# Pair 0 of a fused attention and MLP kernel: its loads on GpSimd's queue, other staging slots, an earlier shift flag, an earlier copy of the output weights

## The chip, the cores and the metric

One core of one Trainium2 chip. The metric is the device time of the kernel in microseconds (us), the median of the runs. Engines are named as in the profile: PE is TensorE (matmul), DVE is VectorE, ACT is ScalarE, POOL is GpSimd, SP is SyncE, which only issues transfers. "SPq" and "ACTq" are what an engine's own queue of instructions spends on issuing a transfer.

## The reference

```python
# x: (8, 1024, 512), H = 16 heads of 32, float32
y = layernorm(x)
q, k, v = split(y @ w_qkv)                       # per head; q and k are halved into q1,q2 and k1,k2
a = softmax(q1 k1^T / sqrt(32)) - lam * softmax(q2 k2^T / sqrt(32))
out = a @ v                                      # rms-normed over the 32 columns, times norm_w * 0.2
x = x + reshape(out) @ wo
z = layernorm(x)
h = bitlinear(z, w_fc) + gate * (z @ v.T @ fast_b.T @ u.T)   # bitlinear: ternary weights with a row scale
x = x + bitlinear(relu(h) ** 2, w_proj)
```

## The kernel before

Everything runs in one program with an order written out by hand for each engine; semaphores join them. Matmuls of float32 precision are made of three products of a high and a low part (`fp32r`).

**Opening.** The rows of x are taken in chunks of 512. For chunks 0 and 1 (batch 0) the kernel makes 24 "tiles" T = 0..23, twelve a chunk: eight tiles of q and k (numbered Q = 0..15 over both chunks) and four of v (V = 0..7). Each tile is 12 matmuls on PE (`pe_tile`, L822 for q and k, L825 for v) into one of four PSUM banks, T % 4, then a copy on ACT (`act_tile`), which takes the high part (L1286) or v (L1291), then for q and k the low part on DVE (`dve_low`, L1621) and the largest magnitude (`dve_bound`, L1631). SP then stores the tile into scratch tensors in DRAM (`sync_store`, L514 for q and k, L524 for v). Chunk 1 makes its tiles Q = 8..15 at T = 12..19 and V = 4..7 at T = 20..23. Between them PE also turns chunk 2 (`pe_turn`, ACT L1249, DVE L1571), and ACT and DVE quantize `w_fc`.

**The main loop** runs over 64 pairs of heads, P = 0..63, each in steps d = 0..7 of two score blocks. For block gg = 16 P + k, PE makes scores in two halves c = 0 and 1 (`pe_score`, L884; half 0 is in banks 0 and 1, half 1 in banks 2 and 3), ACT takes the exponential of each half (`act_exp`, L1308) into one of four slots of the tensor `pr`, gg % 4, DVE adds each block of a half pair to `acc` (`dve_add`, L1687, seven adds for eight blocks), and PE multiplies the block by v (`pe_pv`, L909). After seven adds PE sums `acc` over the partitions (`pe_sum`, L932). Between them lie the tiles of later batches (three tiles a pair from T = 24; tile 24 has six matmuls in d = 0 and six in d = 1), layer norm of a later chunk (DVE L1588: four statistics of chunk 3 in P = 0, d = 1), and the output projection of earlier pairs. The last stage is the MLP.

**What joins the opening to pair 0.** The scores of pair P read `qst` and `kst`, which are loaded from the scratch tensors by eight transfers (`sync_load_qk`, L552 and L554), and `pe_pv` reads `vst`, loaded in two halves (`sync_load_v`, L565): rows 0 to 3 of blocks before k = 0 is used, rows 4 to 7 before k = 4. In SP's order the q and k loads of pair 0 stand after the store of T = 15, the first half of v after T = 16, the second half after all 24 stores. Then come the loads of pair 1. A flag tells if pair 0 needs a shift of its scores against overflow: DVE takes the magnitudes (`dve_flag(0, 0)` after T = 19), PE spreads them (`pe_flag`, L839, inside T = 20), DVE makes the flag and zeroes `mh` (`dve_flag(0, 1)`, L1644 to L1651), and ACT issues four transfers from `mh` into two rows of `qst` (`sync_shift`, L576). The first score waits for these, for the loads, and for ACT's reads of all four PSUM banks (`s_v` at 8).

**Memory shared in time.** The eight staging slots `stp` of Q = 0..15 lie in the same SBUF memory as the four slots of `pr`: block gg = 0..3 of pair 0 overwrites staging slots 2 gg and 2 gg + 1. So `act_exp` for blocks 0 to 3 waits until the stores of the two tiles in these slots have landed. Before the change tile Q lies in slot (Q + 6) % 8:

```python
def stage(Q):
    return stp[:, (Q + 6) % STG] if Q < 16 else stg[:, Q % 2]
...
for slot in range(2 * gg, 2 * gg + 2):
    Q = STG + (slot + 2) % STG          # blocks 0..3: Q = 10,11 / 12,13 / 14,15 / 8,9
    stored(e, Q)
```

The output weights are cast on ACT by one instruction (L1443, `woh`) after the copy of tile T = 22, and DVE takes the low part (`wol`, L1849) before its first add. GpSimd fills rows of `kst` with ones at the start (slot 0) and after the fourth quantized unit (slot 1, L370); its next work is the layer norm of chunk 3 (L484).

Of the kernel before, what the change touches and what calls it, by code (L numbers as in the profile page):

```python
# [102 lines left out]
def build(nc, x, wqkv, wo, lq1, lq2, lk1, lk2, norm_w, fast_b, w_fc, w_proj, u, v, gate, out):  # L103
# [10 lines left out]
    with ExitStack() as top:  # L114
# [117 lines left out]
        with ExitStack() as al:  # L232
# [39 lines left out]
        s_shift = [sem(f"s_shift{k}") for k in range(RING)]  # L272
        s_va = [sem(f"s_va{k}") for k in range(RING)]
        s_vb = [sem(f"s_vb{k}") for k in range(RING)]
        s_wf = [sem(f"s_wf{k}") for k in range(4)]
# [38 lines left out]
                             "s_dn", "s_dfin", "s_fo", "s_res"))  # L314

        def stage(Q):

            return stp[:, (Q + 6) % STG] if Q < 16 else stg[:, Q % 2]

# [3 lines left out]

        def stored(e, Q):

            if Q < 16:
                e.wait_ge(s_stp[Q % STG], 32 * (Q // STG + 1))
            else:
                e.wait_ge(s_stg[Q % 2], 32 * (Q // 2 - 7))

# [20 lines left out]
        def gpsimd_program(e):  # L351
# [13 lines left out]
            for hh in range(2):  # L365
                e.wait_ge(s_pool, 7 + hh)
                e.memset(kst[64 * hh + 32:64 * hh + 64, 0, :, :].bitcast(F32), 1.0).then_inc(s_pool, 1)
            e.wait_ge(s_tern, 4)
            for hh in range(2):
                e.memset(kst[64 * hh + 32:64 * hh + 64, 1, :, :].bitcast(F32), 1.0).then_inc(s_k1, 1)  # L370

            for P in range(LOWP - 1):
                if P - 1 in JOINED:
                    join_halves(e, P - 1)
                if SUM_P <= P < PROJ_P:
                    pool_magnitudes(e, 2 * (P - SUM_P))
                if PROJ_P <= P < PROJ_P + 16:
                    pool_ternary(e, P - PROJ_P)
                pool_part_apply(e, P)
                if SUM_P <= P < PROJ_P:  # L380
                    pool_magnitudes(e, 2 * (P - SUM_P) + 1)
                if P - 1 in POOLED:
                    pool_normed(e, P - 1)
                if P == PROJ_P + 16:
                    e.wait_ge(s_tts, 16 * 24)
                    e.memset(fba[:], 0.0).then_inc(s_pool, 1)
# [116 lines left out]
        def sync_store_qk(e, b, c, i):  # L503
            m, Q = TILES[i], (2 * b + c) * 8 + i
            sc = (qsc if m < 4 else ksc)[b % 2, m % 4]
            e.wait_ge(s_qh, Q + 1)
            e.wait_ge(s_ql, Q + 1)
            if c == 0 and b >= 2:

                last = (b - 2) * NP + 2 * (m % 4)  # L510
                e.wait_ge(s_ring[last % 2], 128 * (last // 2 + 1))
                e.wait_ge(s_ring[(last + 1) % 2], 128 * ((last + 1) // 2 + 1))
            for part in range(2):
                e.dma_start(sc[:, part, :, c * 512:(c + 1) * 512], stage(Q)[:, part, :].bitcast(F32)) \  # L514
                    .then_inc(s_stp[Q % STG] if Q < 16 else s_stg[Q % 2], 16)

        def sync_store_v(e, b, c, st):
            t, V = 4 * c + st, (2 * b + c) * 4 + st
            e.wait_ge(s_v, V + 1)
            if b >= 2 and t in (0, 4):  # L520
                last = (b - 1) * NP - 1
                for r in range(RING):
                    e.wait_ge((s_vb if t else s_va)[r], 16 * ((last - 1 + (last - 1 + r) % 2) // 2 + 1))
            e.dma_start(vsc[b % 2, :, t].rearrange("p q d -> p (q d)"), stage_v(V)).then_inc(s_vsg[V % 2], 16)  # L524
# [8 lines left out]

        def sync_load_qk(e, P):
            b, q = divmod(P, NP)
# [12 lines left out]
            for dst, sc, both, again in ((qst, qsc, 0, 32), (kst, ksc, 16, 0)):  # L548
                for hh in range(2):
                    rows = sc[b % 2, tile, s0 + 2 * hh:s0 + 2 * hh + 2]  # L550
                    r0, r1 = 64 * hh + both, 64 * hh + again
                    e.dma_start(dst[r0:r0 + 32, r, :, :].bitcast(F32), rows.rearrange("j c d s -> (c d) j s")) \  # L552
                        .then_inc(s_ring[r], 16)
                    e.dma_start(dst[r1:r1 + 16, r, :, :].bitcast(F32), rows[:, 0].rearrange("j d s -> d j s")) \  # L554
                        .then_inc(s_ring[r], 16)

        def sync_load_v(e, P, half):
            b, q = divmod(P, NP)
# [4 lines left out]
            if P >= RING:  # L563
                e.wait_ge(s_pv, 16 * (P - RING) + 16)
            e.dma_start(vst[:, r, t0:t0 + 4, :], vsc[b % 2, :, t0:t0 + 4, q, :]).then_inc((s_vb if half else s_va)[r], 16)  # L565

# [116 lines left out]
        def sync_program(e):  # L683
# [12 lines left out]
            for T in range(24):  # L696
# [7 lines left out]
                if T in (10, 22):  # L704
                    sync_x(e, 2 if T == 10 else 3)
                if T == 15:
                    sync_load_qk(e, 0)
                if T == 16:
                    sync_load_v(e, 0, 0)
            sync_load_v(e, 0, 1)  # L710
            for P in range(NPAIR):
                w, more = P // 4, 3 * P + 24 < 24 * B
                for d in range(8):
                    if d == 0 and P + 1 < NPAIR:
                        sync_load_qk(e, P + 1)
                    if d == 6 and P + 1 < NPAIR:
# [3 lines left out]
                    if d in (2, 7) and P + 1 < NPAIR:  # L720
                        sync_load_v(e, P + 1, d // 7)
                    if d == 7 and w + 4 < NC + 2:
# [123 lines left out]
        def pe_shift(e, flag, P):  # L846

            r, base_pe, base_dve, b0 = P % RING, 33 * P, 34 * P, shift_bank(P)
            with e.If(flag > 0):
                e.wait_ge(s_ring[r], 128 * (P // RING + 1))  # L850
                if P:
# [20 lines left out]
        def pe_score(e, P, k, c):  # L872
            gg, j, t, r = 16 * P + k, k // 8, k % 8, P % RING
            if k == 0 and c == 0:
                e.wait_ge(s_ring[r], 128 * (P // RING + 1))
                e.wait_ge(s_shift[r], 64 * (P // RING + 1))
            if gg:
                e.wait_ge(s_exp, n_half(gg - 1, c))
            elif c == 0:
                e.wait_ge(s_ql, 16)  # L880
                e.wait_ge(s_v, 8)
            for hh in range(2):
# [5 lines left out]
        def pe_pv(e, gg):  # L888
# [3 lines left out]
            if k == 0:  # L892
                e.wait_ge(s_va[r], 16 * (P // RING + 1))
            if k == 4:
                e.wait_ge(s_vb[r], 16 * (P // RING + 1))
            if t == 0:
# [373 lines left out]
        def act_tile(e, T, bk):  # L1270
            C, i = kind_of(T)
            e.wait_ge(s_tile, T + 1)
            if i < 8:
                Q = C * 8 + i
                if Q < 16:
                    if Q == 2:
                        e.wait_ge(s_wl, 8)
                    if Q >= STG:
                        stored(e, Q - STG)
                        e.wait_ge(s_qx, Q - STG + 1)  # L1280
                elif Q >= 18:
# [11 lines left out]
        def act_exp(e, P, k, c):  # L1293
# [3 lines left out]
            if c == 0:  # L1297
# [4 lines left out]
                else:  # L1302

                    for slot in range(2 * gg, 2 * gg + 2):
                        Q = STG + (slot + 2) % STG
                        stored(e, Q)
# [104 lines left out]
        def scalar_program(e):  # L1411
# [9 lines left out]
            for T in range(24):  # L1421
# [15 lines left out]
                if T - 2 in UNIT_AT:  # L1437
                    act_ternary(e, UNIT_AT.index(T - 2))
                if T == 22:
                    e.wait_ge(s_wo, 16)  # L1440
# [357 lines left out]
        def vector_program(e):  # L1798
# [16 lines left out]
            for T in range(24):  # L1815
# [24 lines left out]
                if T == 19:  # L1840
                    dve_flag(e, 0, 0)
                if 0 <= k < 4:
                    dve_turn(e, C + 1, k, 4 + k)
                if T == 20:
                    dve_flag(e, 0, 1)
                    flag = load_flag(e, 0)
                    dve_shift(e, flag, 0)
            e.wait_ge(s_woh, 1)
            e.tensor_tensor(wol[:], wos, woh[:], ALU.subtract).then_inc(s_wol, 1)  # L1849
# [163 lines left out]
```

## Time and profile before

| | us |
|---|---|
| median of 3 runs | 3742.93 (3742.35 to 3745.72) |
| profiled execution | 3746.0 |
| its span (first to last instruction) | 3743.9 |
| PE busy in the span | 3704.6 (99%) |
| DVE / ACT / POOL busy | 3149.4 / 2789.7 / 721.1 |
| granted TensorE clock, mean | 0.998 |

Times of rows are microseconds from the span's start. A busy row of PE can hold waits inside: matmuls are pipelined and their ends are modelled. The profiled execution's time is the span and 2.1 us around it.

### The profile page before, as it was taken

To read this page: it belongs to the slowest core of one execution; us is meant where nothing else is said; L and a number is where in the kernel's file an instruction comes from. 1 tells how busy PE (TensorE), PEld (TensorE's weight loads), DVE (VectorE), ACT (ScalarE), POOL (GpSimd) and SP (SyncE) were. 2 spreads that over 40 slices of the span, in tenths; PEclk is the share of its full clock that TensorE was granted. 3 is DMA by queue.
4 is the path that set the end of the run, shared out by engine and by line. 5 is a ranking of instruction groups with operands and counts; after the bars stand their busy time and mean duration, and the time that the engine had idled before them with its cause. 6 is when DMAs were issued, how large, how long until landed. Compare 5 with 4: busy or idle time off the path is not lost.

```text
span 3743.9 us, 57714 instructions
## 1 busy us (share of the span) xinstructions
PE 3704.6 (99%) x21736; PEld 2054.7 (55%) x21736; DVE 3149.4 (84%) x2886; ACT 2789.7 (75%) x3614; POOL 721.1 (19%) x325
## 2 busy tenths in 40 slices
PE   8999999999999999999999999999999999999999
PEld 6344444444444444444444444444468888888887
DVE  6899999999999999999999999988875555555554
ACT  4898888988888888888888888889873333333333
POOL 0101101024545445234332401320020000000000
PEclk9999999999999999999999999999999999999999
DMA  7544444445444544554555444544340101010010
GB/s 241 133 102 102 107 104 104 105 99 111 101 101 103 110 106 99 111 112 104 116 110 116 98 98 103 128 93 114 78 152 23 46 23 46 23 45 23 29 40 23
DMA packets 247207, 344.58 MB, mean 92 GB/s; under 512 B 118048, under 2 KB 126240, under 8 KB 245856
## 3 DMA queue, kind: packets, MB, share of 16 engines
q1 hardware_dynamic: 243360, 324.43, 36.8%
q0 software_dynamic: 3392, 15.73, 1.3%
q8 instruction: 208, 3.41, 0.4%
q14 instruction: 119, 0.97, 0.1%
q10 hardware_dynamic: 128, 0.03, 0.0%
HBM read 198.55 MB, written 131.07 MB: 88 GB/s over the span
## 4 chain that ended last, share of the span: by engine, by line
PE 92%; DVE 4%; issue 1%; ACT 1%; SPq 1%; DMA 0%; DVEq 0%; ACTq 0%
PE ps L909 23%; PE ps L884 17%; PE ps L978 13%; PE ps L1036 12%; PE ps L822 9%; PE ps L964 5%; PE ps L825 4%; PE ps L932 3%; DVE acc L1687 3%; PE ps L983 2%; PE ps L786 1%; PE ps L1072 1%; PE ps L945 1%; ACT pr L1308 1%; PE ps L1057 1%
## 5 line engine op out<-in xcount | busy, mean ns | idle before, releaser
L1308 ACT ACTIVATE pr<-ps 128x1024 f32<-128x1024 f32 x2048 | 1989.7, 1029 | 261.0 <-PE ps L884 252.1
L1687 DVE TENSOR_TENSOR acc<-acc,pr 128x2048 f32<-128x2048 f32 x768 | 1788.3, 2328 | 43.6 <-ACT pr L1308 14.6
L909 PE MATMUL ps<-pr,vst 128*32 128x512 f32 x8192 | 1009.1, 598 | 0.0
L884 PE MATMUL ps<-qst,kst 50*128 50x512 f32 x4096 | 781.2, 456 | 11.5 <-ACT pr L1308 9.7
L884 PEld LDWEIGHTS ps<-qst,kst 50*128 50x128 f32 x4096 | 336.9, 184 | 659.3 <-ACT pr L1308 462.7
L909 PEld LDWEIGHTS ps<-pr,vst 128*32 128x32 f32 x8192 | 213.1, 109 | 445.8 <-issue 437.8
L1478 ACT ACTIVATE rb<-ps,scf 128x512 f32<-128x512 f32 x228 | 157.1, 689 | 349.5 <-PE ps L983 349.5
L1036 PE MATMUL ps<-tP,hh_ 128*128 128x512 f32 x1024 | 399.4, 390 | 1.4 <-DVE hl_ L1911 1.4
L1036 PE MATMUL ps<-tP,hl_ 128*128 128x512 f32 x1024 | 398.8, 389 | 0.0
L822 PE MATMUL ps<-xt,wqh 128*128 128x512 f32 x1024 | 379.3, 423 | 1.4 <-ACT xt L1253 0.8
L484 POOL TENSOR_SCALAR xin<-xin,mv,rs 128x512 f32<-128x512 f32 x60 | 206.5, 3445 | 868.1 <-DVE rs L1606 868.1
L978 PE MATMUL ps<-yh,tT 128*128 128x512 f32 x896 | 350.9, 392 | 0.0
L978 PE MATMUL ps<-yl,tT 128*128 128x512 f32 x896 | 348.7, 389 | 0.0
L1687 DVE TENSOR_TENSOR acc<-pr 128x2048 f32<-128x2048 f32 x128 | 294.7, 2302 | 52.2 <-ACT pr L1308 49.6
L822 PEld LDWEIGHTS ps<-xt,wqh 128*128 128x128 f32 x1024 | 191.3, 191 | 118.9 <-issue 81.6
L1036 PEld LDWEIGHTS ps<-tP,hh_ 128*128 128x128 f32 x1024 | 192.2, 188 | 43.5 <-DVE hl_ L1911 2.3
L1036 PEld LDWEIGHTS ps<-tP,hl_ 128*128 128x128 f32 x1024 | 192.2, 188 | 39.9 <-issue 0.2
L822 PE MATMUL ps<-xt,wql 128*128 128x512 f32 x512 | 203.7, 399 | 0.0
L1906 DVE TENSOR_TENSOR sb2a<-rb 128x512 f32<-128x512 f32 x114 | 78.8, 691 | 137.2 <-ACT rb L1478 137.2
L825 PE MATMUL ps<-wqh,xt 128*128 128x512 f32 x512 | 190.0, 417 | 0.0
L978 PEld LDWEIGHTS ps<-yl,tT 128*128 128x128 f32 x896 | 168.3, 188 | 34.1
L978 PEld LDWEIGHTS ps<-yh,tT 128*128 128x128 f32 x896 | 168.2, 188 | 34.1
(183 smaller groups left out, 3900.1 us busy)
## 6 DMA issues: line engine op xcount, KB each, us to landing
qst<-q_scratch SPq DMA_DIRECT2D x128, 256.0 KB, 4.6
kst<-k_scratch SPq DMA_DIRECT2D x128, 256.0 KB, 7.1
q_scratch<-stg SPq DMA_DIRECT2D x112, 256.0 KB
k_scratch<-stg SPq DMA_DIRECT2D x112, 256.0 KB
qst<-q_scratch SPq DMA_DIRECT2D x128, 128.0 KB, 5.0
kst<-k_scratch SPq DMA_DIRECT2D x128, 128.0 KB, 7.6
vst<-v_scratch SPq DMA_DIRECT2D x128, 128.0 KB, 4.8
xr<-in_L_attn_x_dram SPq DMA_DIRECT2D x64, 256.0 KB
```

The lines of the kernel that those rows point to most:

```text
L484: e.tensor_scalar(xin[:, st, :], xin[:, st, :], mv[:, st, 0:1], rs[:, 8 + st:9 + st], ALU.subtract, ALU.mult) \
L822: t = e.matmul(ps[:, bk, :], w[:, k, m0:m0 + 128], xx[:, k, :], start=(n == 0), stop=(n == 11))
L825: t = e.matmul(ps[:, bk, :], xx[:, k, st * 128:(st + 1) * 128], w[:, k, 2 * E:3 * E], start=(n == 0), stop=(n == 11))
L884: ins = e.matmul(ps[:, 2 * c + hh, :], kst[rows, r, j, t * 128:(t + 1) * 128], qst[rows, r, j, c * 512:(c + 1) * 512], start=True, stop=True)
L909: ins = e.matmul(ps[32 * c4:32 * c4 + 32, 4 + j, :], vst[:, r, t, 32 * hh:32 * hh + 32], pr[:, sl, c, hh, :], start=(t == 0), stop=(t == 7 ...
L932: t = e.matmul(ps[32 * c4:32 * c4 + 32, sum_bank(X, j), :], ones[:], acc[:, j, (2 * c + hh) * 512:(2 * c + hh + 1) * 512], start=True, sto ...
L964: t = e.matmul(ps[:, 7, :], o_[:, kk, :], w_[:, kk, :], start=(kk == 0 and i == 0), stop=(kk == 3 and i == 2))
L978: t = e.matmul(ps[:, bk, :], tT[:, i, m // 2, :], (hi, lo)[m % 2][:, m // 2, :], start=(m == 0), stop=False)
L1036: t = e.matmul(ps[:, rt, :], h_[:, uu % 3, rt * 128:(rt + 1) * 128], tP[:, i, :], start=(i == 0 and part == 0), stop=(i == 15 and part == 1))
L1308: e.activation(pr[:, sl, c, :, :], ps[:, 2 * c:2 * c + 2, :], ACT.Exp, scale=SCALE).then_inc(s_exp, 1)
L1478: e.activation(rb[:, uu % 2, :], ps[:, 4 + uu % 2, :], ACT.Relu, scale=scf[:, 0, i:i + 1]) \
L1687: e.tensor_tensor(acc[:, j, :], old, new, ALU.add).then_inc(s_add, 1)
```

## The change

Four edits that belong to the opening and pair 0:

1. **Slots.** Tiles Q = 8..15 lie in slots 0..7 in order, so blocks 0..3 of pair 0 wait for the stores of Q = 8,9 / 10,11 / 12,13 / 14,15. Tiles Q = 0..7 keep their slots; a tile of chunk 1 waits for the tile of chunk 0 that had its slot.
2. **Loads of pair 0.** GpSimd issues the eight loads of q and k and the first half of v after it has filled slot 0 of `kst` with ones, and the second half of v after it has filled slot 1. They have semaphores of their own. SP issues none of them; after the 24 stores it goes on to the loads of pair 1.
3. **Flag.** In DVE's step T = 20 the flag and `mh` come before the turn of chunk 2's last quarter, not behind it.
4. **Output weights and banks.** ACT casts `wo` after T = 21 instead of T = 22. The first score's half 0 waits for ACT's reads of banks 0 and 1 only (`s_v` at 6), half 1 for all (8).

```diff
+        def ring_of(P):
+            return (s_ring[P % RING], 128 * ((P + 1) // RING)) if P else (s_first, 128)
+        def values_of(P, half):
+            return ((s_vb if half else s_va)[P % RING], 16 * ((P + 1) // RING)) if P else (s_vfirst[half], 16)
+        def slot_of(Q):
+            return Q - STG if Q >= STG else (Q + 6) % STG
         def stage(Q):
-            return stp[:, (Q + 6) % STG] if Q < 16 else stg[:, Q % 2]
+            return stp[:, slot_of(Q)] if Q < 16 else stg[:, Q % 2]
...
         # gpsimd_program, behind the ones of kst slot 0
+            load_qk(e, 0)
+            load_v(e, 0, 0)
             e.wait_ge(s_tern, 4)
             for hh in range(2):
                 e.memset(kst[64 * hh + 32:64 * hh + 64, 1, :, :].bitcast(F32), 1.0).then_inc(s_k1, 1)
+            load_v(e, 0, 1)
...
         # sync_program
-                if T == 15:
-                    sync_load_qk(e, 0)
-                if T == 16:
-                    sync_load_v(e, 0, 0)
-            sync_load_v(e, 0, 1)
...
         # pe_score
             elif c == 0:
                 e.wait_ge(s_ql, 16)
+                e.wait_ge(s_v, 6)
+            else:
                 e.wait_ge(s_v, 8)
...
         # act_tile
                     if Q >= STG:
-                        stored(e, Q - STG)
-                        e.wait_ge(s_qx, Q - STG + 1)
+                        last = (slot_of(Q) + 2) % STG
+                        stored(e, last)
+                        e.wait_ge(s_qx, last + 1)
...
         # act_exp, blocks 0 to 3
                     for slot in range(2 * gg, 2 * gg + 2):
-                        Q = STG + (slot + 2) % STG
+                        Q = STG + slot
                         stored(e, Q)
                         e.wait_ge(s_qx, Q + 1)
...
         # scalar_program: the cast of wo
-                if T == 22:
+                if T == 21:
...
         # vector_program
                 if T == 19:
                     dve_flag(e, 0, 0)
-                if 0 <= k < 4:
-                    dve_turn(e, C + 1, k, 4 + k)
                 if T == 20:
                     dve_flag(e, 0, 1)
                     flag = load_flag(e, 0)
                     dve_shift(e, flag, 0)
+                if 0 <= k < 4:
+                    dve_turn(e, C + 1, k, 4 + k)
```

The rest of the diff gives the waits on `s_ring`, `s_va` and `s_vb` their new form (`ring_of`, `values_of`), renames `sync_load_qk` and `sync_load_v` to `load_qk` and `load_v`, and numbers `s_stp` by slot.

## Rows read from the trace of the kernel before

**Rows 1.** The page: the span and the first engine's busy time.
```profile
span 3743.9 us, 57714 instructions
...
PE 3704.6 (99%) x21736; PEld 2054.7 (55%) x21736; DVE 3149.4 (84%) x2886; ACT 2789.7 (75%) x3614; POOL 721.1 (19%) x325
```

**Rows 2.** The chain that ended last, 65 to 125 us: start, us, what.
```profile
97.47 9.97 DMA k_scratch<-stp
```

**Rows 3.** PE's timeline: start, duration, instruction, count, idle time before and its releaser.
```profile
97.12 0.39 PE L825 MATMUL ps<-wqh,xt 128*128 128x512 f32 x1
99.22 0.73 PE L884 MATMUL ps<-qst,kst 50*128 50x512 f32 x4 [1.72 <-DMA qst<-mh]
100.83 0.50 PE L884 MATMUL ps<-qst,kst 50*128 50x512 f32 x2 [0.88 <-ACT pr L1308]
...
103.78 1.22 PE L884 MATMUL ps<-qst,kst 50*128 50x512 f32 x4
...
118.05 1.92 PE L909 MATMUL ps<-pr,vst 128*32 128x512 f32 x16
...
128.88 1.06 PE L932 MATMUL ps<-acc,ones 128*32 128x512 f32 x8
```

**Rows 4.** ACT's timeline around the first exponentials.
```profile
92.39 2.63 ACTq L576 DMA_DIRECT2D qst<-mh  x4
...
96.09 1.92 ACT L1443 ACTIVATE woh<-acc 128x2048 fp32r<-128x2048 f32 x1
...
102.49 1.02 ACT L1308 ACTIVATE pr<-ps 128x1024 f32<-128x1024 f32 x1 [0.80 <-DMA k_scratch<-stp]
104.61 1.02 ACT L1308 ACTIVATE pr<-ps 128x1024 f32<-128x1024 f32 x1 [1.10 <-PE ps L884]
107.62 2.94 ACT L1308 ACTIVATE pr<-ps 128x1024 f32<-128x1024 f32 x3 [1.99 <-DMA k_scratch<-stp]
```

**Rows 5.** DVE's timeline, from tile 15's low part to the third add of pair 0.
```profile
85.82 0.69 DVE L1621 TENSOR_TENSOR stp<-ps,stp 128x512 fp32r<-128x512 f32 x1 [1.31 <-ACT stp L1286]
...
87.42 0.68 DVE L1571 TENSOR_TENSOR xt<-ps,xt 128x512 fp32r<-128x512 f32 x1
...
91.18 0.27 DVE L1651 MEMSET mh<- 32x256 f32 x1
...
105.67 2.29 DVE L1687 TENSOR_TENSOR acc<-pr 128x2048 f32<-128x2048 f32 x1 [5.34 <-ACT pr L1308]
109.59 2.29 DVE L1687 TENSOR_TENSOR acc<-acc,pr 128x2048 f32<-128x2048 f32 x1 [1.63 <-ACT pr L1308]
112.88 0.69 DVE L1621 TENSOR_TENSOR stg<-ps,stg 128x512 fp32r<-128x512 f32 x1 [0.99 <-ACT stg L1286]
...
115.86 2.27 DVE L1687 TENSOR_TENSOR acc<-acc,pr 128x2048 f32<-128x2048 f32 x1
```

**Rows 6.** SP's timeline: the last stores of the opening and the loads behind them.
```profile
100.68 0.62 SPq L489 DMA_DIRECT2D xin<-in_L_attn_x_dram  x1
101.34 2.35 SPq L524 DMA_DIRECT2D v_scratch<-stg  x1
112.66 0.37 SPq L565 DMA_DIRECT2D vst<-v_scratch  x1
```

**Rows 7.** Loads of half of v (L565), 0 to 140 us, and their time to landing.
```profile
L565 SPq DMA_DIRECT2D vst<-v_scratch x4: 370/392/573, 89.2 to 135.8; - x4
...
DMA to landing us min/median/max: 2.5/5.5/10.6
```

**Rows 8.** GpSimd's own transfers late in the kernel: issue times, and landing of the four.
```profile
2416.26 2.37 POOL L401 DMA_DIRECT2D tT<-tt_scratch  x4
...
DMA to landing us min/median/max: 11.3/15.0/18.4
...
L473 POOL DMA_DIRECT2D rbl<-r_scratch x28: 536/536/584, 2732.7 to 2797.7; - x28
```

**Rows 9.** Windows: stretch, length, busy of the engines, granted clock, DMA share, GB/s.
```profile
100.00:110.00 10.00, 6.95 (x25) 3.39 (x26) 3.03 (x3) 6.12 (x7) 0.00 (x0) 0.75 0.88 306
```

## The prediction before the run

> **What bounds the kernel now.** I read the page first: PE is busy 3704.6 of 3743.9 us [rows 1], so in the long middle nothing but less PE work or less PE idling helps, and the change removes no matmul. What it can win lies in the 39.3 us that PE is not busy, and in matmuls that run slowly. The change touches only the seam between the opening and pair 0, so I went on to the chain of work that ended last, in the stretch 65 to 125 us. It runs on SP's queue, which issues one store of q and k after another with other transfers between them, until the last one, of tile 15, has been issued at 97.47 and takes 9.97 us to land [rows 2]. Then it jumps to ACT.
>
> The ACT timeline shows why. The exponential of block 2 writes where tile 15 is staged, and starts at 107.62, after an idle 1.99 us put down to that store; block 1 had waited 0.80 us for tile 13's store at 102.49 [rows 4]. PE's timeline shows the same from its side: the tiles end at 97.12 + 0.39 = 97.51, the first score starts at 99.22 after 1.72 us for the transfer of `mh`, and there are waits again later [rows 3]. In the window 100 to 110 us PE is busy 6.95 of 10 us, at a mean granted clock of 0.75, between the two levels of 1.2 and 2.4 GHz; PE had idled just before [rows 3, 9].
>
> The DVE timeline tells what the lost time is worth. Its first add starts at 105.67 after 5.34 us of idling, the second at 109.59 after 1.63, the low part of tile 24 at 112.88 after 0.99, and from there DVE works without a gap through the third add at 115.86 [rows 5] up to PE's sum at 128.88 [rows 3], which needs the seventh add. From the sum on, PE is full. So the gain is how much earlier DVE reaches the third add with its blocks ready.
>
> **The change part by part.**
>
> *Flag.* `dve_turn` of the last quarter (0.68 us, as its like in [rows 5]) and the wait for ACT ahead of it are taken from the flag's way. PE's flag matmuls were over at about 88.2, DVE's turn of the third quarter ends at 87.42 + 0.68 = 88.1. The zeroing of `mh` starts 91.18 [rows 5]; three small instructions stand ahead of it (0.56 us), so it can start at 88.25 + 0.56 = 88.8. ACT issues the four transfers 1.21 us behind that start now (92.39 against 91.18), so at 90.0, where ACT is just through with its copy for the turn. They take 2.63 us [rows 4], to 92.65, and the last now lands at about 99.2, 4.8 us after its own issue at 94.3 [rows 3, 4]; then at 96.8. That is ahead of PE's 97.51. The first score's limit becomes the end of the tiles. Cost: the turn of the last quarter comes perhaps 0.5 us later, in a stretch where DVE idles for microseconds; without that cover it would be 0.5 us.
>
> *Output weights and banks.* The cast of 1.92 us stands now at 96.09 [rows 4], ahead of the copy of the last tile. Behind T = 21 it starts at 92.65 + 0.6 = 93.25 and ends 95.2, in ACT's idle time. V = 6 follows at 95.2, V = 7 when PE is through at 97.55, to 98.15. Half 0 of the first score can start at 97.5, half 1 at 98.2. `wol` on DVE (2.29 us) ends at 97.5, well before any add. All of this is hidden; the visible part is the 1.6 us by which the first exponential moves: 98.15 instead of 99.75.
>
> *Slots.* Blocks 1 and 2 no longer wait for tiles 13 and 15. Block 3 waits for tile 15. Its low part is ready at 86.5 (the row at 85.82 lasts 0.69 [rows 5]), and SP is free of the nine loads that it issued between 81.08 and 89.6, so I take its issue at 87 to 90 in place of 97.47; with the 9.97 us of [rows 2] it lands by 100. Block 3 starts near 105.4, so this wait goes away, with 5 us to spare. In the opening, tiles 8 to 15 now wait for other tiles of chunk 0; the tightest is tile 13 at 73 for tile 7, whose store was issued at 56.45 to 57.6. With the 9.97 us it lands by 67.6. Cost nothing.
>
> *From there to the third add.* Exponentials take 1.02 us, some 0.95 back to back. Block 0: 98.15 and 99.1. Block 1, half 0: 100.0. For half 1, PE has the score of half 0 at 99.25 (when block 0's half is read), six matmuls of tile 24, then the score. That took 103.78 - 100.83 = 2.95 us plus 0.83 to the exponential at 104.61 [rows 3, 4], at the lower clock for most of it. At the higher clock the six are 1.0 us shorter. PE's idle times ahead shrink from 2.60 us (1.72 + 0.88 in [rows 3]) to about 0.8, so I take the middle: 99.25 + 3.3 = 102.5, ends at 102.0 and 103.0. First add: 103.5 (now 105.67). Second add: 103.5 + 2.29 = 105.8 (block 2 is ready at 105.4). Tile 24's copy on ACT comes at about 107.2, so DVE's low part starts when the second add ends, at 108.1, where now 112.88. The four statistics need x of chunk 3: its load is issued at about 96.4 instead of 100.68 [rows 6] and took 11.4 us, so 107.8, in time. The third add starts 2.98 us after the low part, as now (115.86 - 112.88): 111.1. That is 4.8 us less; by the ends of the clock term 4.3 to 5.3.
>
> *Loads on GpSimd.* No load from this queue at this place exists in the trace. The nearest rows: 28 transfers of 256 KB at 0.54 us an issue, and four of 1 MB issued in 2.37 us, one behind another without waiting for a landing of 11.3 to 18.4 us [rows 8]. Tile 9's store has landed by 81.0, as SP did not wait for it then; by the latest GpSimd issues nine loads from 81.0 to 86. From below, landing as on SP now (3.5 to 9.3 us): 95.3. From above, the 18.4 of [rows 8]: 104.4, which is 6.9 us late. I take the first: the 18.4 belongs to transfers four times as large that queued behind each other. The ones of `kst` slot 1 (3.66 us) move behind these loads, to about 90; they are needed for pair 1's loads after 99. SP's queue loses about 8 us of issuing, and gives it to the stores, as used above. POOL's next work, at 130, is far.
>
> *The second half of v.* Now SP waits 5.7 us for V = 7's store, issued 101.34 and landed after 11.3 us, and issues at 112.66; it lands in 2.5 us, at 115.2; block 4 needs it at about 119 (second half of the row at 118.05) [rows 3, 6, 7]. After: V = 7 is stored at 98.3, lands between 106.5 (a landing of 8) and 109.6 (11.3), GpSimd adds 0.6, the load 2.5 to 10.6 [rows 7]. So it lands between 109.6 and 120.8, and is needed at 119 - 4.8 = 114.2. New is that pair 1's eight loads (1.5 MB), so far behind that wait, are now issued at once behind V = 7 and run beside it. With the median of 5.5 I get 112.6 to 115.7, a wait of 0 to 1.5 us. I charge 0.4.
>
> A rule speaks against this part. In [rows 5] DVE is in an add nearly all the time from 103 on, an instruction with two operands in SBUF. The Trainium skill (SBUF — State Buffer, "Who interferes with whom") says that GpSimd can't write its descriptors while DVE holds the port pair they share; it counts two-operand adds as takers of the read side only and infers that descriptors pass. By that inference the sum stands; if the adds did block, the issue would wait for the end of one add, up to 2.29 us more, and the gain would be about 2.5. No row here has both at once.
>
> **Sum.** 4.8 - 0.4 = 4.4 us. Against the profiled execution, 3746.0, that is 3741.6; that one was 3.1 above the median, so from the median, 3742.93, I forecast **3738.5**. Of this kernel 0.2% is 7.5 us, about what a measurement can tell from no change, and the forecast is within it.
>
> **The rivals.**
> *A. As worked out*, PE's first sum at about 124.5 in place of 128.88: 3737.5 to 3739.6. Chance 0.57.
> *B. The second half of v takes the place of the wait removed.* For it: pair 1's loads beside it and a DMA share of 0.88 at this time now [rows 9]. Against: x is issued earlier too. At a landing of 120.8 PE would wait 6.6 us at block 4, and the whole comes out 1.8 us above now: 3744.7; half way, 3741.4. Chance 0.25 for 3739.6 to 3744.7.
> *C. Slower: GpSimd's loads are late for the first score.* Needed at 97.5; from 99.22 on it loses against now. At the 18.4 us of [rows 8], 104.4: the start is 5.2 later than now, less the 3.2 us that slots still give (4.8 less the 1.6 of the start): +2.0, 3744.9. If each had to land (4.4 us, the median of those 28) before the next is issued, nine take 44 us and the start is at 125: +22.6, 3765.5. For it: nothing in the opening tests that queue. Against: four in flight at once in [rows 8]. It passes 0.2% from a start at 110 on. Chance 0.08, of which 0.05 beyond 0.2%.
> *D. More than forecast*, because PE's clock stays up and ACT and DVE find more slack: the first add can't start before 103, so by DVE's own work 5.3 is the limit, 3737.6; less only by run to run variation. Beyond it, by something I don't see: 0.10, a fifth of it beyond 0.2%.
>
> **How the numbers follow.** The likeliest is A, 3738.5. With A and B's nearer part, and about 1.5 us for how medians of such runs differ, 8 in 10 lie from 3736.3 to 3742.8. Faster by over 0.2% (below 3735.4): 0.04, from D and variation. Slower by over 0.2% (above 3750.4): 0.05, from C. Within: 0.91.
>
> **What would show it.** Right: no wait of ACT L1308 for `k_scratch<-stp`; ACT's four issues at about 90; the first score at 97.6; adds at 103.5, 105.8, 111.1; the first L932 at 124.5; the granted clock of 100 to 110 above 0.75. Wrong: PE L909 waiting for `vst` near 114 (B); the first score waiting for `qst` or `kst` loads (C); DVE's statistics waiting for `xin`.

## The result and the profile after

| | before | after |
|---|---|---|
| median, 22 runs each | 3743.34 | 3748.45 |
| lowest to highest | 3741.18 to 3746.96 | 3746.09 to 3753.35 |
| profiled execution / its span | 3746.0 / 3743.9 | 3748.61 / 3746.9 |

The ratio is 1.0013, 95% interval 1.0008 to 1.0019. The kernel is 5.1 us slower, where 4.4 us faster was forecast. It is less than the 0.2% that a measurement was taken to tell, but with 22 runs it is clear of zero. The two profiled executions differ by less, 2.6 us, because that of the kernel before ran 2.7 us over its median and that of the kernel after 0.2.

PE's timeline of the kernel after (the first score, the products with v of blocks 3 and 4 with the wait between them, the first sum; L895, L920 and L943 answer to L884, L909 and L932 of [rows 3]):

```profile
96.28 0.50 PE L895 MATMUL ps<-qst,kst 50*128 50x512 f32 x2
...
110.42 1.07 PE L920 MATMUL ps<-pr,vst 128*32 128x512 f32 x8
120.36 1.94 PE L920 MATMUL ps<-pr,vst 128*32 128x512 f32 x8 [8.88 <-DMA vst<-v_scratch]
...
131.47 1.04 PE L943 MATMUL ps<-acc,ones 128*32 128x512 f32 x8
```

PE starts the first score 2.9 us sooner than in [rows 3] and, at block 3's product (110.42), is 7.6 us ahead of 118.05. Then it stands still for 8.88 us, for the second half of v, and makes the first sum at 131.47 instead of 128.88. DVE's timeline after has the same turn, with another wait in it:

```profile
101.57 2.29 DVE L1699 TENSOR_TENSOR acc<-pr 128x2048 f32<-128x2048 f32 x1 [5.21 <-ACT pr L1320]
103.97 2.29 DVE L1699 TENSOR_TENSOR acc<-acc,pr 128x2048 f32<-128x2048 f32 x1
106.18 0.68 DVE L1633 TENSOR_TENSOR stg<-ps,stg 128x512 fp32r<-128x512 f32 x1
112.56 2.47 DVE L1600 BATCH_NORM_STATS2 st<-xin 128x6 f32<-128x512 f32 x4 [5.70 <-DMA xin<-in_L_attn_x_dram]
114.94 2.27 DVE L1699 TENSOR_TENSOR acc<-acc,pr 128x2048 f32<-128x2048 f32 x1
```

The queues show where both come from. SP's timeline after, then GpSimd's:

```profile
96.77 0.43 SPq L503 DMA_DIRECT2D xin<-in_L_attn_x_dram  x1
97.25 1.31 SPq L538 DMA_DIRECT2D v_scratch<-stg  x1
98.81 0.39 SPq L566 DMA_DIRECT2D qst<-q_scratch  x1
...
102.25 0.44 SPq L568 DMA_DIRECT2D kst<-k_scratch  x1
```

```profile
78.66 0.50 POOL L568 DMA_DIRECT2D kst<-k_scratch  x1
91.76 0.81 POOL L579 DMA_DIRECT2D vst<-v_scratch  x1 [12.61 <-issue]
92.61 3.66 POOL L383 MEMSET kst<- 32x2048 f32 x2
113.52 0.76 POOL L579 DMA_DIRECT2D vst<-v_scratch  x1 [17.25 <-DMA v_scratch<-stg]
```

Tile V = 7's store is issued at 97.25, 4.1 us sooner than in [rows 6]. Pair 1's eight loads follow at 98.81 to 102.7; in [rows 6] SP was stuck until 112.66 and they came behind that. Now the store takes 15.9 us to land (11.3 before), the load of x 15.8 (11.4 before), GpSimd can issue at 113.52, and its load lands 6.7 us later, at 120.2. The store lands 0.6 us behind x (112.0 and 112.6 before, 112.5 and 113.1 now). The windows (their last three columns: granted clock, DMA share, GB/s) show the transfers' side and the price on the clock:

```profile
100.00:105.00 5.00, 4.62 (x27) 2.14 (x26) 3.32 (x2) 4.14 (x5) 0.00 (x0) 1.00 1.08 314
105.00:110.00 5.00, 5.00 (x34) 2.39 (x32) 1.86 (x2) 4.00 (x5) 0.00 (x0) 1.00 1.09 157
110.00:115.00 5.00, 1.48 (x12) 0.20 (x10) 2.44 (x5) 1.94 (x2) 0.76 (x1) 0.95 0.95 127
115.00:120.00 5.00, 0.00 (x0) 0.00 (x0) 4.96 (x9) 0.50 (x2) 0.00 (x0) 0.50 0.58 172
120.00:125.00 5.00, 4.64 (x16) 1.89 (x16) 3.58 (x3) 1.94 (x2) 0.00 (x0) 0.53 0.17 56
```

The DMA engines are full from 100 to 115 us. During PE's standstill the granted clock falls to 0.50, the lower level of 1.2 GHz, and stays there into the next window (0.53); the eight matmuls at 120.36 take 1.94 us where eight at 110.42 took 1.07.

### The profile page after: what moved, and what is told of

The parts are those of the page before. It is cut to its first block, busy times and chain, and to the rows that moved or that the text cites. A ratio compares the mean times of both kernels' runs of the same rounds, so it can differ in the third digit from the quotient of the medians.

```text
span 3746.9 us, 57714 instructions
## 1 busy us (share of the span) xinstructions
PE 3704.0 (99%) x21736; PEld 2054.0 (55%) x21736; DVE 3149.4 (84%) x2886; ACT 2790.5 (74%) x3614; POOL 728.9 (19%) x335
## 4 chain that ended last, share of the span: by engine, by line
PE 90%; DVE 5%; issue 2%; ACT 1%; DMA 1%; ACTq 0%; SPq 0%; DVEq 0%; POOLq 0%
PE ps L920 23%; PE ps L895 17%; PE ps L989 13%; PE ps L1047 12%; PE ps L831 9%; PE ps L975 5%; PE ps L834 4%; DVE acc L1699 4%; PE ps L943 3%; PE ps L994 2%; PE ps L795 1%; PE ps L1083 1%; PE ps L956 1%; PE ps L1068 1%; ACT pr L1320 1%
## 5 line engine op out<-in xcount | busy, mean ns | idle before, releaser
L920 PE MATMUL ps<-pr,vst 128*32 128x512 f32 x8192 | 1010.2, 599 | 8.9 <-DMA vst<-v_scratch 8.9
L895 PE MATMUL ps<-qst,kst 50*128 50x512 f32 x4096 | 781.5, 456 | 7.4 <-ACT pr L1320 7.1
L895 PEld LDWEIGHTS ps<-qst,kst 50*128 50x128 f32 x4096 | 337.1, 184 | 655.7 <-ACT pr L1320 458.8
L920 PEld LDWEIGHTS ps<-pr,vst 128*32 128x32 f32 x8192 | 213.0, 109 | 455.0 <-issue 444.5
```

The source lines that it names most:

```text
L895: ins = e.matmul(ps[:, 2 * c + hh, :], kst[rows, r, j, t * 128:(t + 1) * 128], qst[rows, r, j, c * 512:(c + 1) * 512], start=True, stop=True)
L920: ins = e.matmul(ps[32 * c4:32 * c4 + 32, 4 + j, :], vst[:, r, t, 32 * hh:32 * hh + 32], pr[:, sl, c, hh, :], start=(t == 0), stop=(t == 7 ...
```

## The experiments

Two theories at first. **Theory 1**: the order costs the time. SP's own load of the second half of v, which waited for V = 7's store, held back pair 1's loads; with it on GpSimd they start 10 us early and slow that store and what comes after it. **Theory 2**: GpSimd's queue is slow by itself. "First sum" is the start of pair 0's first L932 (or its line in that kernel) in the one profiled execution; "median" stands against that of the kernel before beside it, measured in the same set. The ratio is the record's own for the runs of both kernels; it is not the quotient of the two medians.

| kernel | first sum | median, its before | ratio (95%) |
|---|---|---|---|
| before | 128.9 | | |
| after | 131.5 | 3748.45, 3743.34 | 1.0013 (1.0008 to 1.0019) |
| e1_gate | 125.5 | 3741.99, 3744.18 | 0.9998 (0.9989 to 1.0007) |
| e2_all_sp | 125.1 | 3743.34, 3744.18 | 1.0001 (0.9992 to 1.0010) |
| e3_gpsimd_only | 130.3 | 3748.75, 3744.18 | 1.0014 (1.0005 to 1.0023) |
| e4_v2_sp | 124.1 | 3739.51, 3744.18 | 0.9988 (0.9979 to 0.9997) |
| e5_x_early | 123.2 | 3740.43, 3743.29 | 0.9997 (0.9988 to 1.0006) |
| e6_slots_only | 124.6 | 3742.98, 3743.29 | 1.0002 (0.9993 to 1.0011) |
| e7_v7_first | 128.1 | 3746.09, 3743.29 | 1.0009 (1.0000 to 1.0018) |
| e10_sp_order | 133.0 | 3750.84, 3743.82 | 1.0020 (1.0011 to 1.0029) |
| e12_gate_landed | 122.1 | 3741.42, 3743.82 | 0.9993 (0.9984 to 1.0002) |
| e13_flag_banks | 126.1 | 3745.83, 3743.82 | 1.0006 (0.9997 to 1.0015) |
| e15_gate_landed_2 | 124.0 | 3740.53, 3743.79 | 0.9991 (0.9982 to 1.0000) |
| e16_v2_sp_2 | 122.0 | 3741.14, 3743.79 | 0.9993 (0.9984 to 1.0002) |
| e17_all_sp_2 | 128.1 | 3743.16, 3743.79 | 0.9994 (0.9985 to 1.0003) |

**e1_gate.** After, with SP held until V = 7's store has landed:

```diff
         # sync_program, behind the 24 stores
+            e.wait_ge(s_vsg[1], 64)
+            e.wait_ge(s_vsg[0], 64)
             for P in range(NPAIR):
```

> The changed kernel, and SP waits for the stores of v (tile V = 7) before it issues pair 1's loads, as it did by its place in the order before. Theory 1 (pair 1's 1.5 MB, issued at 98.8 us right behind V = 7, slow its store from 11.3 to 15.9 us): the store lands about 11 us after 97.3, so at 108 to 109, GpSimd's load of the second half of v lands by 113 to 116, PE waits 0 to 3 us for it instead of 8.9, the first L932 of pair 0 comes at 125 to 127 and the median is 3738 to 3741. Theory 2 (GpSimd's path is slow by itself, the store's landing is not pair 1's doing): the store still takes 15 to 16 us, PE waits 8 to 9 us, 3748.

The store took 12.2 us instead of 15.9, GpSimd issued at 108.48, v landed 5.5 us later, PE waited 3.4 us for it instead of 8.9. The wait list of PE in e1_gate, 90 to 140 us (total, times, longest):

```profile
PE ps L897 <- ACT pr L1322: 3.7, 8, 0.9
PE ps L922 <- DMA vst<-v_scratch: 3.4, 1, 3.4
```

For theory 1. With two added waits on SP the median is 2.2 us below that of the kernel before, where the change had put it 5.1 above; by its interval e1_gate is no different from the kernel before.

**e2_all_sp.** Edits 1, 3 and 4; all of pair 0's loads on SP at their old places (`load_qk(e, 0)` after T = 15, `load_v(e, 0, 0)` after T = 16, `load_v(e, 0, 1)` after the stores).

> Edits 1, 3 and 4 alone: slots, flag, weights and banks; SP issues all loads of pair 0 at their old places. Theory 1: SP's own load of the second half of v gates pair 1's loads again; SP's backlog returns too (V = 7's store at 98 to 101). PE waits 0 to 2 us for v, first L932 at 125 to 127, 3738.5 to 3741. Theory 2 expects the same here: it can't be told apart by this run. A third theory, that the time is lost elsewhere in the three edits: 3746 or more.

The profile came as forecast, the median hardly moved. So the other three edits don't lose the 5 us; what they gain is less than forecast. e17 returns to it.

**e3_gpsimd_only.** Edit 2 alone; slots, flag, weights and banks as before.

> Edit 2 alone on the kernel before: GpSimd issues pair 0's loads, slots, flag, weights and banks stay. Theory 1: stores are issued earlier (no wait of ACT for tile 15), but pair 1's loads come behind V = 7 at once; second half of v lands at about 120, PE waits for it some 5 to 8 us, 3746 to 3750. Theory 2: the same. If the loss needs the other three edits: 3740 to 3743.

Slower by 4.6 us: nearly the whole loss is in this one edit. V = 7's store took 14.8 us, PE waited 5.2 us for v.

**e4_v2_sp.** After, with one line moved back:

```diff
         # gpsimd_program
-            load_v(e, 0, 1)
...
         # sync_program, behind the 24 stores
+            load_v(e, 0, 1)
```

> The changed kernel, with only the second half of v back on SP at its old place, ahead of pair 1's loads; GpSimd issues q, k and the first half. Theory 1: as e1_gate, and 0 to 3 us sooner by the landing (2.5 us before): PE waits 0 to 1.5 us, first L932 at 124.5 to 126, 3737.5 to 3740. Theory 2 (GpSimd's path): also good, but then e1_gate stays at 3748. So the pair e1_gate and e4_v2_sp tells them apart.

Its interval leaves 1 out, at 0.9988: the best median of all (in its second set, e16_v2_sp_2, the interval holds 1). GpSimd still issues nine of pair 0's ten loads, so these do no harm beyond a wait of 0.5 us for the first of PE's products with v, which starts at 99.95, when the first half of v has just landed (99.9). SP's timeline shows the old order again, with the second half of v ahead of pair 1:

```profile
97.09 2.46 SPq L537 DMA_DIRECT2D v_scratch<-stg  x1
109.30 0.37 SPq L578 DMA_DIRECT2D vst<-v_scratch  x1
109.91 0.54 SPq L565 DMA_DIRECT2D qst<-q_scratch  x1
```

The store took 12.2 us, the load 2.1.

**e5_x_early, e7_v7_first.** The load of chunk 3's x is moved in SP's order (`if T in (10, 22)` becomes `(10, 20)` on e4_v2_sp and `(10, 23)` on the kernel after).

> e4_v2_sp (second half of v back on SP ahead of pair 1's loads) with the load of chunk 3's x issued after T = 20 instead of T = 22. In e4_v2_sp DVE waited 2.2 us for that load and its first L932 came at 124.1. If the transfers' order alone sets these waits: x lands about 3 us sooner, DVE's wait is gone, V = 7's store lands as before (12 us after its issue), first L932 at 122.5 to 124, median 3737.5 to 3739.5. If the queue is simply full at this time: V = 7 lands later by as much as x lands sooner, the second half of v is late instead, 3739.5 to 3742.

> The changed kernel, with chunk 3's x load issued after V = 7's store instead of before it; pair 1's loads still follow at once, and GpSimd loads the second half of v. If V = 7's store is late because of what is issued behind it (pair 1's 1.5 MB): it still takes 13 to 16 us, v lands at 117 or later, PE waits 6 us or more, DVE waits longer for x, 3747 to 3751. If it is late because of the 1 MB of x ahead of it: it lands by 106 to 108, v by 112 to 115, PE waits 0 to 3 us, and 3741 to 3745.

In e5_x_early DVE no longer waited for x, the first sum was at 123.2, and the median no different from e4_v2_sp's by more than they scatter. In e7_v7_first both my branches were half right: V = 7's store landed in 6.9 us, with pair 1's loads and x behind it, and GpSimd could issue at 104.46. So the store is quick without x ahead of it. x itself still took 14.6 us, beside pair 1's loads. But the load of v, issued beside pair 1's loads, then took 12.3 us instead of 6.7, PE waited 5.3 us, DVE 5.1 for x, and the kernel stayed slower. So pair 1's loads cost twice: they lengthen x's load, behind which V = 7's store lands, and GpSimd's load of v. In e7_v7_first the first packet of that load started only at 113.0, 8.6 us after its issue, against 1.5 to 2.0 us in the other runs; what held it there is not shown.

**e12_gate_landed, e15_gate_landed_2.** One step beyond e1_gate; SP waits until the second half of v has landed:

```diff
+            e.wait_ge(s_vfirst[1], 16)
             for P in range(NPAIR):
```

> The changed kernel, all of pair 0's loads on GpSimd, and SP holds pair 1's loads until the second half of v has landed, not only until tile V = 7 is stored (e1_gate, where v took 5.5 us to land and PE waited 3.4). Theory 1 in its second part (pair 1's loads also slow GpSimd's load of v beside them): v lands in 3 to 4 us, PE waits 0.5 to 2 us, first L932 at 124 to 125.5, 3739 to 3742. If the 5.5 us are GpSimd's own: PE waits 3.4 us as in e1_gate, 3742.

> e12_gate_landed once more. Its profile had the first L932 at 122.1, 6.8 us ahead of the kernel before, but its median was only 2.4 us lower. If the saved time stays to the end and the first median was chance: 3737 to 3740. If part of it is given back later in the timed runs: 3740.5 to 3742.5 again.

GpSimd's load landed in 3.2 us and PE didn't wait for it; in e15_gate_landed_2 it landed in 2.7 us and PE waited 0.7 us. The waits of PE in e12_gate_landed, 90 to 150 us, and its window 105 to 110:

```profile
PE ps L896 <- ACT pr L1321: 3.1, 7, 0.9
PE ps L944 <- DVE acc L1700: 1.2, 1, 1.2
```

```profile
105.00:110.00 5.00, 5.00 (x34) 2.43 (x32) 4.97 (x7) 3.82 (x5) 0.76 (x1) 1.00 0.15 46
```

The DMA share is 0.15 where it was 1.09 in the kernel after, and theory 2 is out: this is GpSimd's queue, all ten loads on it, in its best order, with medians 2.4 and 3.3 us below that of the kernel before (each interval still reaches 1). It is as good as e4_v2_sp within what these runs can tell.

**e10_sp_order.** The converse: no load on GpSimd at all (e2_all_sp), but SP issues pair 1's loads ahead of pair 0's second half of v:

```diff
-            load_v(e, 0, 1)
             for P in range(NPAIR):
...
                     if d == 0 and P + 1 < NPAIR:
                         load_qk(e, P + 1)
+                        if P == 0:
+                            load_v(e, 0, 1)
```

> No load on GpSimd: edits 1, 3 and 4, all loads of pair 0 on SP, but pair 1's eight loads are issued ahead of pair 0's second half of v, so they no longer wait for tile V = 7's store. Theory 1 (the order, not GpSimd, costs the time): V = 7's store takes 14 us or more instead of 10.8 (e2_all_sp), the second half of v lands at 117 or later, PE waits 5 us or more for it, first L932 at 128 or later, 3746 to 3750. Theory 2 (GpSimd's queue is the cause): as e2_all_sp, first L932 at 125, 3741 to 3744.

7.0 us slower than the kernel before, the slowest of all. SP and PE in e10_sp_order:

```profile
95.76 2.34 SPq L535 DMA_DIRECT2D v_scratch<-stg  x1
98.34 0.50 SPq L563 DMA_DIRECT2D qst<-q_scratch  x1
...
111.65 0.38 SPq L576 DMA_DIRECT2D vst<-v_scratch  x1
```

```profile
119.39 1.94 PE L923 MATMUL ps<-pr,vst 128*32 128x512 f32 x8 [8.65 <-DMA vst<-v_scratch]
```

The store took 15.9 us again, the load of v 7.6, and PE waited 8.65 us, without GpSimd. This is the cause on its own.

**e6_slots_only, e13_flag_banks.** The other edits by themselves, all loads on SP: edit 1, and edits 3 and 4.

> Edit 1 alone (slots), all loads of pair 0 on SP as in the kernel before. By my sum the slots are worth 4.8 less the 1.6 us that the earlier start gives, 3.2 us: first score at 99.2 after a wait for the transfers of the shift rows, no wait for tile 15's store, first L932 at 126 to 127, median 3740 to 3742. If flag, weights and banks carry the gain: as the kernel before, 3743 to 3744.

> Edits 3 and 4 alone (flag, output weights, banks); slots as before, all loads on SP. The first score comes at about 97.6 or sooner, but block 2 still waits for tile 15's store at about 105 to 107.5, so by my sum nearly nothing reaches the first L932: 127 to 129, 3742 to 3744. If these edits carry a gain of their own: 125 to 126.5.

Slots alone gave a first sum at 124.6, earlier than I had them (126 to 127), yet a median within 0.3 us of that of the kernel before; the part on the prediction says how the two go together. Flag, weights and banks alone started the first score early and then waited for tile 15's store, in ACT's wait list of e13_flag_banks (95 to 125 us):

```profile
ACT pr L1322 <- DMA k_scratch<-stp: 2.9, 2, 2.7
```

A first sum at 126.1, a median 2.0 us higher with an interval that holds 1. No gain of their own.

**e8_v_first, e14_q_v_k.** GpSimd's order: first half of v first, or between the q and the k loads. They ask why that load was held 12.61 us in the kernel after.

> The changed kernel with GpSimd's first load of v ahead of its eight loads of q and k. In the changed kernel that load, ninth on the queue, was issued 12.6 us behind the eighth, just after the eighth had landed, with no wait of its own left. Theory: the queue had no room for its 512 pieces of 256 bytes until the loads ahead had landed. Then here v is issued at about 75 and the last of the eight loads wait for it (several us of idling between issues, the last issued at 82 or later). If the 12.6 us belong to the v load itself (a late store), v comes at 75 or later without delay, and the eight follow back to back, the last at 80 to 81.

> The changed kernel with GpSimd's first load of v between its four loads of q and its four of k. In e8_v_first, v went first at 66.8 without delay and the eight followed back to back after it had landed; in the changed kernel, ninth behind eight in flight, it was held 12.6 us. Theory (the queue has room for only so many pieces in flight): v behind four in flight is held until those four have landed or nearly so (6 to 9 us, issued at 80 to 84), or it fits, and then the loads of k are held. If instead v is never held behind four and k follows at once, room is not the reason.

In e8_v_first it was issued at 66.8, before the tiles for q and k were stored; it had landed (75.6) before the third of the eight went out, they followed back to back, and nothing was held. My times for it were wrong, and it shows only that its own wait is over by 66.8. In e14_q_v_k v went fifth without delay, and the ninth load, one of k, was held. GpSimd's timeline of e14_q_v_k:

```profile
75.25 0.80 POOL L580 DMA_DIRECT2D vst<-v_scratch  x1
76.03 0.54 POOL L567 DMA_DIRECT2D kst<-k_scratch  x1
...
87.07 0.51 POOL L569 DMA_DIRECT2D kst<-k_scratch  x1 [9.48 <-issue]
```

So the ninth load waits, whichever it is, and not for a semaphore of its own. That it lacks room in the queue is argued, and what counts as room is open: in e14_q_v_k the first load had landed at 78.0, and the hold went on until 87.07, 0.4 us after the landing of v (86.7), with one load of k still under way. Both kernels kept the fault of the change, one run each: 3749.5 and 3746.8.

**e16_v2_sp_2, e17_all_sp_2.** e4_v2_sp and e2_all_sp again.

> e4_v2_sp once more: 4.7 us lower by its median, first L932 4.8 us ahead. If the median follows the first sum, again 3738.5 to 3740.5, and ahead of e15 by nothing or behind it by 1 to 2 us.

> e2_all_sp once more. Its profile had 1.6 us more than the kernel before between the first and the second L932, in a stretch where the granted clock fell to 0.72 (140 to 145 us). If that belongs to this kernel: again, first L932 at 125, second at 146.5 to 147, 3742 to 3743.5. If it comes and goes from run to run: second L932 at 145.3 in this profile, or the median at 3739.5 to 3741.5.

e4_v2_sp was lower by 4.7 and 2.7 us in its two sets, e2_all_sp by 0.8 and 0.6, e12_gate_landed by 2.4 and 3.3. The first sums of two executions of one kernel differ by 2 to 3 us (e2_all_sp 125.1 and 128.1, e4_v2_sp 124.1 and 122.0): one profile doesn't fix them closer. And what is saved at the first sum doesn't always stay. e2_all_sp's windows before its second sum, and e4_v2_sp's for the same stretch:

```profile
140.00:145.00 5.00, 5.00 (x25) 1.74 (x22) 4.78 (x3) 2.27 (x4) 0.00 (x0) 0.72 0.98 180
```

```profile
140.00:145.00 5.00, 5.00 (x38) 2.27 (x34) 4.40 (x4) 3.65 (x4) 0.00 (x0) 1.00 0.99 179
```

The granted clock fell to 0.72 in the one and not in the other. From the first to the second sum it is 21.9 us in both profiles of e2_all_sp, 21.7 to 21.9 in e1_gate, e8_v_first, e13_flag_banks, e14_q_v_k and e15_gate_landed_2, and 20.2 to 20.3 in before, after, e3_gpsimd_only, e4_v2_sp twice, e5_x_early, e6_slots_only, e7_v7_first, e10_sp_order and e12_gate_landed. That is 1.6 us given back. It doesn't belong to a kernel: e12_gate_landed and e15_gate_landed_2 are the same, and the clock of 140 to 145 us was 1.00 in the one (20.2 us) and 0.70 in the other (21.7 us). So it is not shown to be the reason why e2_all_sp gains less than e4_v2_sp; and in their second sets the ratios, 0.9994 and 0.9993, don't tell the two apart.

## Why the prediction was wrong

- **Which part bound the kernel**: right. The seam between the opening and pair 0 moved with the store of tile 15. After the change no wait of ACT for it is left in 95 to 125 us.
- **Flag, weights and banks**: right. ACT's four issues came at 88.88 (90.0 forecast), the first score at 96.28 (97.5), half 1 at 97.03 behind ACT's read. The opening of that execution was itself 1.2 us shorter, so this is the forecast to 0.1 us.
- **Slots, to the third add**: the forecast had adds at 103.5 and 105.8, measured 101.57 and 103.97, low part 106.18 (108.1). The third add, forecast at 111.1, came at 114.94, behind the wait for x. PE's clock stayed at 1.00 through 110 us; I had halved that term.
- **The loads of q, k and the first half of v on GpSimd** cost nothing in the kernel after, as forecast: those of q and k were issued from 74.9 to 79.2, the last landed by 91.4, before the first score. The first half of v was held, issued at 91.76, and landed at 97.5; PE used it from 100.63 on. The margin is small: in e4_v2_sp the hold cost 0.5 us. Rival C fell.
- **The step that failed is "The second half of v"**: its landing of V = 7 in 8 to 11.3 us, and the charge of 0.4 us. The upper bound came from an execution in which nothing stood behind that store. I named what was new, that pair 1's eight loads now follow at once, and then left it out of both the store's landing and x's: 15.9 and 15.8 us. PE waited 8.88 us where I had 0 to 1.5, so the charge should have been the whole forecast gain and more. e10_sp_order and e12_gate_landed show the cause from both sides. The term that the loads lengthen first is x: in all 15 runs with x right ahead of V = 7 the store landed 0.6 to 0.8 us behind x, and with x behind it (e7_v7_first) it took 6.9 us. I also misread how long SP stood: two waits of 5.7 and 3.2 us, 8.9 in all and not 5.7.
- **x of chunk 3** was called in time at 107.8; DVE waited 5.70 us for it, to 112.56. The same omission, at the same place.
- **Rival B** was the right one, and its worst case priced too low. Its landing of 120.8 was met (120.2). Its wait of 6.6 us was 8.9, because PE got there at 111.5 and not at 114.2: the better the other edits work, the longer this wait. And it had no term for the clock: 0.50 to 0.53 from 115 to 125 us. At the first sum this is 0.8 us more than its worst case (131.47 against 128.88 + 1.8). The larger part of the way from 3744.7 to 3748.45 is the base: the rows of before, and their first sum, are of an execution 2.7 us over its median, while I set what I had worked out from them against the median. I gave it 0.25, and the range ended at 3742.8 although this case reached 3744.7.
- **The rule on GpSimd's descriptors and DVE** was not in play at the load for which I raised it. GpSimd issued the second half of v at 113.52, when DVE was in its statistics (112.56 to 115.03), with one operand and no add; in e12_gate_landed it was the same. Nor is DVE in an add nearly all the time in [rows 5]: from 103 us to the third add at 115.86 two adds of 2.29 us stand there. The Trainium skill (SBUF — State Buffer, "Who interferes with whom") infers that two-operand adds don't hold descriptors up, and other rows agree as far as the issue goes: in e1_gate and e15_gate_landed_2 the first half of v was issued (92.23 and 92.92) inside the subtraction for `wol`, which reads two operands in SBUF (91.77 to 94.06 and 91.88 to 94.17). The issue took 0.81 us, as in the kernel after with DVE idle, and the load landed in 5.5 and 5.7 us (5.8 there). Its first packet came 0.4 and 0.6 us later after the issue than there, so a small delay is not ruled out.
- **What is saved at the first sum stays**: right, within one execution. After is 2.6 us behind at the first sum and 2.9 at 2713 us. The time of the profiled execution less the start of its first sum is 3616.4 to 3618.5 us in the ten profiles whose second sum came 20.2 to 20.3 us behind the first (before among them, 3617.1), and 3618.2 to 3620.2 in the seven where it came 21.7 to 21.9 behind. But one profile is one execution. That of before was 2.7 us over its median, and since its time from the first sum on is like the others', the excess lies ahead of it: by estimate the median execution of before has its first sum at about 126.2 (128.9 - 2.7). So e6_slots_only is 4.2 us ahead in the table and 0.3 in its median: its profiled execution took 3742.35 us and that of before 3746.0, 3.7 of the 4.2. The gain that I read from the rows of before may have been too large for the same reason; with the fault mended the medians are 2.4 to 4.7 us below before (e4, e12, e15, e16), where I had 4.4.

## What to carry to other kernels

A wait in an issue queue may be holding back what stands behind it, to everyone's good. When a waiting transfer is moved to another queue, list what its old queue now issues at once, and add those bytes to the landing time of the transfers in flight then, on both queues: here first of the large one (x), and so of the small one that lands behind it. A landing time is a row of the traffic around it, not of the transfer. If the moved transfer is urgent, give the old queue the wait by name: one `wait_ge` turned a loss of 5 us into medians 2.4 and 3.3 us below the kernel before. And before a gain of a few us is read from one profile, compare that execution's time with the median: here it stood 2.7 us over it, by the estimate above ahead of the row that was read.

## What the runs showed of the hardware

- Transfers issued later on the same queue slow a large one issued earlier: x's load of 1 MB landed in 10.2 to 12.4 us with nothing behind it but V = 7's store (before, e1, e2, e4, e6, e12, e13, e15, e16, e17), and in 14.6 to 15.8 with pair 1's 1.5 MB behind it too (after, e3, e7, e8, e10, e14). The 256 KB of V = 7 landed 0.6 to 0.8 us behind x wherever they stood right behind it: 8.7 to 12.2 us after their issue in the first group, 14.5 to 15.9 in the second. Ahead of x (e7_v7_first) they took 6.9 us.
- A load of 128 KB of v issued by SP, with pair 1's loads 0.6 us behind it on the same queue, landed in 2.1 to 2.7 us. Issued by GpSimd it took 2.7 and 3.2 us alone (e15, e12), 5.5 with pair 1's loads issued at the same time (e1), 6.1 to 7.4 with them ahead (after, e3, e8, e14), and 12.3 in e7_v7_first. In the traces the load is 512 packets of 256 bytes on SP's queue and 32 packets of 4 KB on GpSimd's.
- GpSimd's queue took eight loads back to back and held the ninth for 9.5 to 14.1 us, in each of the ten runs that had eight under way: until 0.4 us after the last of them had landed, but in e14_q_v_k with one still under way. In e4_v2_sp and e15_gate_landed_2 the held load, the first half of v, landed within 0.1 us of the start of PE's first product with it.
- Where the granted clock fell to between 0.66 and 0.78 in a window of 5 us from 140 or 145 us on, the stretch from the first to the second sum took 1.5 to 1.7 us longer (e1, e2, e8, e13, e14, e15, e17). It came and went between executions of one kernel (e12 and e15); what sets it is not shown.
